# A decoder layer with cross-attention and a routed feed-forward part: another opening, inputs laid out by the host, and products of the identity on the matrix engine

## The reference

```
x = x + tanh(g_xattn) * attention(layernorm(x), ctx, ctx)   # 16 heads of 16, biases on q, k, v, o
h = layernorm(x) * ln_g + ln_b
logits = h @ Wr                                             # 7 experts
top_vals, top_idx = top_k(logits, 2); gates = softmax(top_vals)
pos = cumulative count of tokens of the same expert; keep = pos < capacity
ye = (silu(xe @ W1) * (xe @ W3)) @ W2                       # per expert, on the gathered tokens
shared = (silu(h @ W1s) * (h @ W3s)) @ W2s
x = x + tanh(g_ffn) * (sum of the gated expert rows + shared)
```

## Time and profile before

| What | Value |
|---|---|
| Median of three runs | 910.91 us |
| The profiled execution | 909.93 us, span 908.2 us |
| TensorE busy | 826.7 us (91%) |
| VectorE, ScalarE, GpSimd busy | 609.4, 385.8, 326.0 us |
| Mean granted TensorE clock | 0.968 |
| VectorE: subtraction of the hidden rows (L1150), product (L1160), one maxima reduction (L1087) | 0.75, 0.68, 0.58 us each |
| VectorE: product of the heads (L1101), shortest and longest in the opening | 0.42 and 1.44 us |
| Half of a shared weight, 512 KB, from issue to landing (W2s, W1s, W3s) | 3.5, 4.1, 4.9 us |

### The profile page before, as it was taken

How to read it: one execution, slowest core, us unless ns; L and a number is a source line. 1 busy time by engine, 2 the same in 40 slices (tenths; PEclk the granted TensorE clock), 3 DMA queues, 4 the chain that set the end, 5 groups by cost and what they waited for, 6 DMA issues and landing times.

```text
span 908.2 us, 14547 instructions
## 1 busy us (share of the span) xinstructions
PE 826.7 (91%) x5130; PEld 713.9 (79%) x5130; DVE 609.4 (67%) x1360; ACT 385.8 (42%) x718; POOL 326.0 (36%) x259
## 2 busy tenths in 40 slices
PE   4766799998999999999899999999999999999991
PEld 3533686885866858758687789999999999999991
DVE  5566877878779778787777766566665656565340
ACT  3254235336344254263535345354444545453330
POOL 5171403104013031040112840846547281823333
PEclk9868799999999999999999999999999999999996
DMA  6542041122400423203113332334434333431111
GB/s 170 139 140 63 10 117 36 44 74 49 117 15 21 116 49 69 56 27 93 36 43 119 110 99 93 83 87 103 85 102 82 86 74 104 97 66 19 16 19 19
DMA packets 97297, 66.93 MB, mean 74 GB/s; under 512 B 57910, under 2 KB 84716, under 8 KB 97240
## 3 DMA queue, kind: packets, MB, share of 16 engines
q1 hardware_dynamic: 43624, 55.40, 21.8%
q0 software_dynamic: 53088, 10.30, 8.3%
q10 hardware_dynamic: 528, 0.52, 0.2%
HBM read 37.38 MB, written 14.27 MB: 57 GB/s over the span
## 4 chain that ended last, share of the span: by engine, by line
PE 68%; DVE 13%; issue 7%; POOL 2%; ACT 1%; DVEq 0%; DMA 0%; POOLq 0%
PE bank L1367 19%; PE bank L1369 18%; PE bank L1368 18%; PE bank L1583 2%; PE bank L1584 2%; PE bank L1585 2%; DVE hidden L1097 2%; PE bank L1448 1%; PE bank L1621 1%; DVE bn_parts L1049 1%; DVE normed_heads L1101 1%; DVE row_max L1087 1%; DVE float_data L1170 1%; PE bank L1549 1%; DVE float_data L1068 1%
## 5 line engine op out<-in xcount | busy, mean ns | idle before, releaser
L1367 PE MATMUL bank<-split_operands 128*128 128x366 f32 (+4 forms) x1148 | 385.7, 336 | 15.2 <-DVE split_operands L1017 9.7
L1368 PE MATMUL bank<-split_operands 128*128 128x366 f32 (+4 forms) x1148 | 379.4, 331 | 0.0
L1369 PE MATMUL bank<-split_operands 128*128 128x366 f32 (+4 forms) x1148 | 379.3, 330 | 0.0
L1367 PEld LDWEIGHTS bank<-split_operands 128*128 128x128 f32 (+1 forms) x1148 | 217.2, 189 | 36.9 <-DVE split_operands L1022 7.2
L1369 PEld LDWEIGHTS bank<-split_operands 128*128 128x128 f32 (+1 forms) x1148 | 216.5, 189 | 12.4
L1368 PEld LDWEIGHTS bank<-split_operands 128*128 128x128 f32 (+1 forms) x1148 | 217.5, 189 | 9.7
L836 POOL DMA_INDIRECT out<-float_data,scatter_now x42 | 125.5, 2987 | 179.6 <-issue 93.0
L1350 DVE TENSOR_TENSOR hidden<-bank,float_data 128x366 f32<-128x366 f32 x112 | 60.4, 540 | 113.9 <-PE bank L1369 113.9
L1003 ACT ACTIVATE float_data<-bank 128x366 f32<-128x366 f32 x112 | 53.5, 477 | 113.7 <-PE bank L1369 113.7
L1000 ACT CAST split_operands<-hidden 128x366 fp32r<-128x366 f32 x112 | 55.7, 497 | 68.4 <-DVE hidden L1350 67.3
L812 POOL DMA_INDIRECT float_data<-z_scratch,gather_now x42 | 72.1, 1718 | 14.9 <-issue 14.0
(11 more groups left out here) (152 smaller groups left out, 1099.9 us busy)
## 6 DMA issues: line engine op xcount, KB each, us to landing
float_data<-in_L_ffn_W SPq DMA_DIRECT2D x21, 1024.0 KB, 8.6
split_operands<-split_operands SPq DMA_DIRECT2D x96, 128.0 KB, 2.3
float_data<-in_x SPq DMA_DIRECT2D x8, 512.0 KB, 4.8
z_scratch<-float_data SPq DMA_DIRECT2D x8, 512.0 KB, 3.1
out<-float_data SPq DMA_DIRECT2D x7, 512.0 KB, 2.8
split_operands<-split_operands SPq DMA_DIRECT2D x8, 192.0 KB, 3.8
float_data<-in_L_ffn_W1s SPq DMA_DIRECT2D x2, 512.0 KB, 4.1
float_data<-in_L_ffn_W3s SPq DMA_DIRECT2D x2, 512.0 KB, 4.9
```

The lines of the kernel that those rows point to most:

```text
L1367: pe.matmul(o, lhs[0], rhs[0], start=first, stop=False)
L1368: pe.matmul(o, lhs[0], rhs[1], start=False, stop=False)
L1369: return pe.matmul(o, lhs[1], rhs[0], start=False, stop=last)
```

## The change

The diff has four parts. (1) The host lays the inputs out: one array for the context, one for the four attention weights, one for all small columns (biases, gains, gates, router weights). Sixteen DMAs of 16 rows for the output weights and seven small ones disappear. (2) The opening's order is written anew; `norm`, `queries` and `project` fall into parts (`stats_x`, `scale_x`, `residual`, `queries_out`, `project_out`). GpSimd takes over two splits of attention weights from VectorE, and the splits of the shared weights are spread. (3) The router of block 0 moves behind the first up products, into `period(1)`. (4) `keep_busy` lets TensorE multiply the identity by itself into a bank that nobody reads: 18 times ahead of the keys, 4 each behind the keys, the transposes, the queries and the second maxima, 8 behind the maxima's transpose.

```
 def first_period(do, b):
     n = b.next()
+    do("keep_busy", 2, 18)
+    do("context")
+    do("weights", 1)
     do("project_keys")
-    do("norm", b)
-    do("keys_lo")
+    do("keep_busy", 2, 4)
+    do("stats_x", b)
+    do("weights", 0)
+    do("scale_x", b)
+    do("bias_keys")
     do("transpose_x", b)
+    do("weights", 2)
+    do("keep_busy", 2, 4)
     do("queries", b)
+    do("keep_busy", 3, 4)
+    do("queries_out", b)
     do("keys", b)
+    do("residual", b)
     do("stack", b)
+    do("shared_weights", 0)
+    for t in range(TT):
+        do("maxima", b, t)
+        if t == 1:
+            do("keep_busy", 6, 4)
+        if t == 2:
+            do("project_values")
     do("maxima_T", b)
+    do("keep_busy", 4, 8)
     do("stack_maxima", b)
+    do("values_out")
+    norm(do, n)
+    do("first_scores", b)
+    do("transpose_x", n)
     do("route_const")
+    do("scores", b, 0)
     do("queries", n)
+    do("scores", b, 1)
+    do("queries_out", n)
     do("stack", n)
...
+    do("shared_weights", 1)
...
     do("stack_maxima", n)
+    do("project_out", b)
     do("norm2", b)
-    do("transpose_z", b)
+    do("shared_rest")
     do("first_scores", n)
-    do("logits", b)
-    do("logits_T", b)
-    do("choose", b)
-    do("norm", n.next())
 def period(do, b):
...
     do("scores", b, 0)
     if b.at(1):
-        do("count", f)
-        do("counted", f)
-        do("slots", f)
+        do("transpose_z", f)
     do("scores", b, 1)
+    if b.at(1):
+        nxt("stats_x")
     up(0)
-    do("place", f)
+    if b.at(1):
+        nxt("scale_x")
+        nxt("residual")
+    else:
+        do("place", f)
     do("attention_hi", b)
+    if b.at(1):
+        do("logits", f)
     up(1)
+    if b.at(1):
+        do("logits_T", f)
     nxt("transpose_x")
     up(2)
     do("project", b)
...
     do("norm2", b)
+    if b.at(1):
+        do("choose", f)
     down(0)
     down(1)
     nxt("maxima", 0)
     up(3)
-    do("transpose_z", b)
-    up(4)
+    if b.at(1):
+        do("count", f)
+        do("counted", f)
+        do("slots", f)
+        up(4)
+        do("place", f)
+        do("transpose_z", b)
+    else:
+        do("transpose_z", b)
+        up(4)
     down(2)
     do("logits", b)
     up(5)
...
+        def keep_busy(j, times):
+
+            if j == 4:
+                pe.wait_ge(sig["m_done"], TT)
+            elif j == 6:
+                pe.wait_ge(sig["xl_ready"], KD)
+            else:
+                pe.wait_ge(sig["ident_ready"], 1)
+            for _ in range(times):
+                pe.matmul(bank[j][:, 0:P], ident[:, :], ident[:, :], start=True, stop=True)
...
         def transpose_x(b):
-            if not (b.at(0) or b.at(1)):
+            if b.at(1):
+                pe.wait_ge(sig["v_ready"], B)
+            elif not b.at(0):
                 pe.wait_ge(sig["attn_done"], b.n * NG)
+            if b.at(2):
+                pe.wait_ge(sig["lg_done"], 1)
...
         def count(b):
             pe.wait_ge(sig["r_onehots"], b.n + 1)
+            if b.at(0):
+                pe.wait_ge(sig["m_done"], 2 * TT + 1)
```

More of the change, by code:

```diff
@@ L429, in build @@
     bvb = af(39, D)[0:SK]
[L430 to L436, removed]
+    small = sb("small_inputs", [P, NSMALL])
+    bq, bk, lng, lnb = (small[:, KD * j:KD * (j + 1)] for j in range(4))
+    gx, gy = small[:, 8:9], small[:, 9:10]
+    wrf = small[:, 10:].rearrange("p (k e) -> p k e", k=KD)
     tgx = sb("tanh_gate_x", [P, 1])
@@ new lines, in load_shared, with first_keys @@
+        def load_shared(h):
+            if h >= 3:
+                sp.wait_ge(sig["wsplit_lo"], NSTEP0 + 2 * (h - 2))
+            if h == 5:
+                sp.wait_ge(sig["xT_ready"], 2 * KD)
+            m, part = h // 2, h % 2
+            kk = wsv[m].shape[1] // 2
+            sp.dma_start(sh_stage[h].rearrange("p (k f) -> p k f", k=kk), wsv[m][:, part * kk:(part + 1) * kk])\
+              .then_inc(shared_loaded[h % 3], 16)
+        for h in range(3):
+            load_shared(h)
+        def first_keys():
+            sp.wait_ge(sig["zeros_ready"], 1)
+            sp.wait_ge(sig["k_hi"], KD)
+            for j in range(8):
+                sp.dma_start(kbd[16 * j:16 * j + 16, :, j, :].bitcast(F32), k_s[16 * j:16 * j + 16, 0, :, 0:SK].bitcast(F32))\
+                  .then_inc(sig["kbd_loaded"], 16)
@@ L586, in project_keys, with more_shared @@
                 sp.dma_start(kscr[j].rearrange("(k p) t -> p k t", p=P), k_s[:, j].bitcast(F32)).then_inc(sig["k_stored"], 16)
-        def load_shared(h):
-            if h >= 3:
-                sp.wait_ge(sig["wsplit_lo"], NSTEP0 + 2 * (h - 2))
-            m, part = h // 2, h % 2
-            kk = wsv[m].shape[1] // 2
-            sp.dma_start(sh_stage[h % 3].rearrange("p (k f) -> p k f", k=kk), wsv[m][:, part * kk:(part + 1) * kk])\
-              .then_inc(shared_loaded[h % 3], 16)
-        for h in range(3):
-            load_shared(h)
-        def load_more_shared(b, half):
-            if b.at(0) and half == 0:
+        def more_shared(half):
+            if half == 1:
                 for h in range(3, 6):
@@ L878, in split_shared, with shared_weights @@
                 m, col = h // 2, (h % 2 * 2 + j) * PIECE
[L879 removed]
+                act.copy(W0[:, 0, m, col:col + PIECE], sh_stage[h][:, j * PIECE:(j + 1) * PIECE])\
                    .then_inc(sig["wsplit_hi"], 1)
+        def shared_weights(half):
+            if half == 0:
+                act.activation(tgx[:, :], gx, ACT.Tanh).then_inc(sig["tanh_done"], 1)
+                act.activation(tgf[:, :], gy, ACT.Tanh).then_inc(sig["tanh_done"], 1)
+            for h in range(3 * half, 3 * half + 3):
+                split_shared(h)
         def transpose_x(b):
@@ L1691, with by_partition @@
     arrays, aps = {}, {}
-    for name, src in [*INS.items(), *((n, n) for n in SAME)]:
-        v = np.asarray(inputs[src])
-        if name.endswith("T"):
-            v = np.swapaxes(v, -1, -2)
+    raw = {n: np.asarray(v) for n, v in inputs.items()}
+    def by_partition(v):
+        return v.reshape(KD, P, -1).transpose(1, 0, 2)
+    rows = np.zeros(D, dtype=np.int64)
+    for h in range(H):
+        rows[feature_at(h):feature_at(h) + DH] = np.arange(h * DH, (h + 1) * DH)
+    att = [raw[f"L0_xattn_W_{c}"].T for c in "qkv"] + [raw["L0_xattn_W_o"].T[rows]]
+    columns = [by_partition(raw[n]).reshape(P, KD) for n in ("L0_xattn_b_q", "L0_xattn_b_k", "L0_ffn_ln_g", "L0_ffn_ln_b")]
+    gates = [np.broadcast_to(raw[n].reshape(1, 1), (P, 1)) for n in ("g_xattn", "g_ffn")]
+    laid_out = {n: raw[n] for n in SAME}
+    laid_out["ctx"] = raw["ctx_1024"].reshape(B, SK, KD, P).transpose(3, 2, 0, 1).reshape(P, -1)
+    laid_out["att"] = np.stack([by_partition(w) for w in att], axis=1)
+    laid_out["small"] = np.concatenate([*columns, *gates, by_partition(raw["L0_ffn_Wr"]).reshape(P, -1)], axis=1)
+    for name, v in laid_out.items():
         v = np.ascontiguousarray(v)
```

350 lines of the change are left out of this document (178 added, 172 removed).

## The result

The changed kernel takes 913.46 us (median of 15 runs, 912.44 to 917.56), the kernel before 911.68 (median of 15, 910.11 to 913.31). The ratio is 1.0024 with a 95% interval of 1.0015 to 1.0033: slower by about 2.2 us. The prediction was 909.0, so even its sign was wrong. The two pages therefore show 4.6 us between the spans where the medians show 1.8.

A forecast was written before the change was run, and what follows sets the result against it. Other waits bound the first 98 us, then TensorE. Block 1's heads at 86.8, plus 6.8 to block 2's transposes and 34.9 onward, end up 5 at 128.5 against 130.4: median 909.0 us, range 904.0 to 914.0.

The forecast's parts named there:

- Keys and identities: Opening, TensorE: 18 identity products end at 8.5 us and delay the keys 1.8; keys' high parts ready at 10.9, as before.
- First scores of block 0: Opening: with SyncE's queue free of small loads, these start at 32.7 us, not 41.54; sign of being right: 31 to 35.
- Block 0's attention: Opening, where GpSimd's chain of splits also delays the exponentials: heads end at 49.9 to 51.8 us, taken as 51, against 61.07.
- To the first scores of block 1: Last shared loads and casts stand ahead of block 1's maxima: scores at 67.5 us against 77.95, 1.6 of gain lost.
- To the heads of block 1: Block 1's attention: up 0 at 81.8 to 86.0 us, heads end at 84.9 to 88.8, mid 86.8.
- What the move costs: Block 0's router among the up products: block 2's transposes to end of up 5 take 34.9 us, against 24.4 before.
- The sum: End of up 5: 86.8 + 6.8 + 34.9 = 128.5 us against 130.4, 1.9 earlier; median 909.0.
- Rival (b): TensorE's lower clock stays through block 1's attention and over place, logits and up 5: heads 88.8, 913.4 us; chance 0.22.
- Rival (a): TensorE at 2.4 GHz early in block 1's attention, clock holding over place: end of up 5 at 125.2, 905.7 us; chance 0.19.
- Rival (c): Opening: identity products at 0.55 us each hold the keys, first scores of block 0 at 35.7, 911.2 us; chance 0.12.
- Rival (d): Opening shortened by 10.8 us and nothing given back, the router's chain fitting beside the up products: 900.1 us; chance 0.03.

## Why the prediction was wrong

- **Keys and identities: right in effect, mis-sized.** 18 products took 5.89 us, 0.33 each, and ended at 7.6; I had 8.5. They delayed the keys by 0.27 us (7.13 without them). SyncE's key copies began at 10.0, not 10.9.
- **First scores of block 0:** 34.0 for 32.7, inside the range given. The queries' copies took 5.78 and 2.52, and the maxima's copy was issued at 31.64, 1.3 late. Right in mechanism.
- **Block 0's attention:** heads at 51.5 for 51. Right.
- **To the first scores of block 1: mis-sized by 2.3 us.** The order that I described was the real one, but the last half landed in time for a cast at 65.85 and not 63.3. The landing was priced right; the queue was not: the queries' copies took 9.07 us on it (49.71 to 58.78) for 7.8, and the last load left it at 60.45 and not 57.8. The terms that I gave (63.3, 1.1, 0.6 and 2.3) also add up to 67.3, not 67.5. I had priced the casts' place as 1.6 us of loss; undoing it brought the scores from 7.3 to 3.6 behind the transposes of the maxima, so it costs 3.7.
- **To the heads of block 1: the step that failed.** I put the heads at 84.9 to 88.8 and took 86.8; they ended at 91.57. 2.3 of the 4.8 come from the step before. The other 2.4 go to the clock: I took the middle between TensorE's two levels, although my own step left TensorE without work for 4.4 us (63.1 to 67.5) just before. It idled 6.69, and the clock was 0.50 from there to 94. The kernel with twenty identities in that wait took 17.2 from scores to heads, the changed kernel 21.8; my sum had 19.3. The wait needn't have been longer than I had it: the kernel without identities idled 4.44 at this place and the one with the maxima ahead 2.98, and both took 21.7 to 21.8. My argument against the low clock, a run from 70 to 77 nearly without gaps, didn't hold either: TensorE was busy 9.60 of the 10 us from 70 to 80, at 0.50 all the while. What would have lifted the clock there stays open.
- **What the move costs: right.** 35.1 from block 2's transposes to the end of up 5 (134.31 − 99.21), 34.9 predicted; count 1.42 for 1.6, place 4.23 for 4.3, logits 1.43 for 2.2. The three waits are 7.1 for 8.1, so some 1 us more than I had went elsewhere in this stretch, and that the sum is met to 0.2 is partly luck. The clock was low behind the wait at place, as I had it (0.58 from 124 to 128). Heads to transposes took 7.6 for 6.8. The kernel with the router put back confirms it from the other side: 11.3 us, where the sum's additions are 10.5 (34.9 − 24.4).
- **The sum.** 4.8 + 0.8 + 0.2 is 5.8: 128.5 became 134.3. In medians the miss is 4.5 (913.46 for 909.0). Rival (b), with 913.4 and the heads behind 88.7 as its condition, is what happened, though the lower clock over place was part of the 35.1 already. The wait for a DMA that I had just worked out and the assumption of a half-fast clock behind it didn't go together, and that wait should have moved the chances to (b).

Rival (a) fell with the heads at 91.57. Rival (c) fell: the identities held nothing and are worth 4.1 us by the medians, 2.6 by the ratios. Rival (d) fell with the router's 11.3; its 10.8 was also mis-taken: it is the difference between up 0 before (97.56) and the end of block 1's heads now (86.8), which are not the same landmark. By block 2's transposes (105.97 and 93.6) it would have been 12.4.

## What to carry to other kernels

Work that is taken out of a stretch with waits and put into one that is full costs its whole chain: here the opening became 8.3 us shorter and the up products 12.2 longer. When a sum yields a wait of several microseconds on TensorE, price the stretch behind it at the lower clock, and look for the instruction that stands in the way in queue order (here a cast that waits for a load, ahead of a copy that everybody waits for). Single gains around one chain don't add up: 3.1, 3.1 and 3.3 gave 5.5, because two of them ended at the same next limit (VectorE's wait for a store), and 3.1 gave nothing once another wait stood in front. Before edits are combined, look for the wait that ends last with each of them in place.

## What the runs showed of the hardware

- VectorE's scaling of 128x256 fp32 rows, memory to memory, took 1356 ns beside GpSimd's subtractions and 408 without them, while GpSimd's took 1293 and 1276. The Trainium skill, SBUF — State Buffer, "SBUF: two separate sides", tells of a lock that the two share; the trace agrees that VectorE is held up beside GpSimd, and shows nothing of GpSimd being held up in turn: VectorE bore all of the loss.
- A product of the identity in fp32 (128 columns, two instructions) took 0.33 us. 42 of them, with no use for their result, made the kernel 4.1 us faster by the medians (2.6 by the ratios). Whether the wait in front of block 1's first scores was filled decided the clock behind it: 1.00 with it and 0.50 without it from 70 to 78 us. That was worth 4.6 us with the scores at 68.5 to 69.8, and nothing with the scores at 66, where VectorE's wait for the store set the heads.
- Behind a wait of 2.98 us (maxima ahead of the casts) the granted clock was 0.50 for 22 us, with TensorE busy 9.60 of the first 10.
- Nine products changed nothing (905.56 and 905.49 us) where a second wait of 4.1 us followed some 4 us behind the first scores.
